# A spare fill between two gathers, no throttle in layer 1, and one activation table set, in a two-layer sparse attention kernel

## The reference

```
q = x @ Wq.T;  k = x @ Wk.T;  v = x @ Wv.T
scores = where(adj.T, q @ k.T, -1e30)
attn   = where(adj.T, softmax(scores, axis=1), 0)
x      = layernorm(x + attn @ v)          # eps 1e-5, no learned scale
```

## Time and profile before

| what | value |
|---|---|
| median of 3 runs | 311.3 us (307.36 to 314.35) |
| the profiled execution | 310.94 us, of which the span 309.1 us |
| PE busy | 186.0 us (60%) |
| ACT busy | 139.9 us (45%) |
| DVE busy | 132.5 us (43%) |
| POOL busy | 94.4 us (31%), of it 91.4 in 96 gathers |
| software DMA queue | 12.59 MB, 15.0% of 16 engines |
| mean granted PE clock | 0.797 of full |

### The profile page before, as it was taken

The page is one execution under the profiler, slowest core; times in us unless marked ns, Lnnn a source line. Parts: engine busy times, 40 slices in busy tenths (PEclk is TensorE's granted clock), DMA queues, the critical chain, the costliest instruction groups (busy, mean ns, idle before and its releaser), DMA issues.

```text
span 309.1 us, 3691 instructions
## 1 busy us (share of the span) xinstructions
PE 186.0 (60%) x1110; PEld 158.4 (51%) x1110; DVE 132.5 (43%) x671; ACT 139.9 (45%) x311; POOL 94.4 (31%) x115
## 2 busy tenths in 40 slices
PE   1739699640185879298878528650583285957640
PEld 1527587530174767197767426450473184946520
DVE  1229557010097780716874201240185063567430
ACT  1012143400124282739999772210245274688884
POOL 3457102777300036000000007776047315610000
PEclk9999685995556678879999968776599559597965
DMA  8999200433200004110011123333013204311112
GB/s 222 325 311 347 88 0 19 103 107 106 77 0 0 3 25 104 42 34 3 33 35 37 34 68 90 108 104 104 4 35 104 69 33 136 89 49 34 36 36 71
DMA packets 20982, 24.92 MB, mean 81 GB/s; under 512 B 2016, under 2 KB 17888, under 8 KB 20960
## 3 DMA queue, kind: packets, MB, share of 16 engines
q0 software_dynamic: 4608, 12.59, 15.0%
q1 hardware_dynamic: 16352, 12.06, 13.0%
HBM read 20.45 MB, written 4.19 MB: 80 GB/s over the span
## 4 chain that ended last, share of the span: by engine, by line
PE 33%; ACT 23%; issue 19%; another core or an unknown queue 16%; DVE 8%; ACTq 0%; DVEq 0%
PE PS L944 8%; PE PS L1056 7%; ACT L451 5%; PE PS L1044 3%; PE PS L1046 3%; PE PS L1009 3%; ACT first_row L424 3%; ACT exps L416 2%; PE PS L935 2%; ACT weight L435 2%; ACT L454 2%; ACT y_sb L443 2%; DVE X L775 1%; PE PS L918 1%
## 5 line engine op out<-in xcount | busy, mean ns | idle before, releaser
L1056 PE MATMUL PS<-WvT,y_sb 128*128 128x256 f32 x128 | 41.4, 456 | 33.0 <-ACT y_sb L443 32.3
L314 POOL DMA_INDIRECT xd<-x_rows,d_row x32 | 30.6, 957 | 98.6 <-DMA x_rows<-X 62.7
L1044 PE MATMUL PS<-ident,both_rows 128*128 128x128 f32 x128 | 32.6, 346 | 25.1 <-DVE both_rows L755 11.7
L944 PE MATMUL PS<-M,xt 128*128 128x256 f32 x128 | 39.5, 463 | 11.7 <-ACT xt L371 8.6
L1056 PEld LDWEIGHTS PS<-WvT,y_sb 128*128 128x128 f32 x128 | 26.0, 222 | 39.8 <-ACT y_sb L443 35.4
L775 DVE SCALAR_TENSOR_TENSOR X<-PS,inv,X 128x256 f32<-128x256 f32 x32 | 15.4, 483 | 66.9 <-PE PS L1056 62.2
L1044 PEld LDWEIGHTS PS<-ident,both_rows 128*128 128x128 f32 x128 | 26.2, 250 | 26.9 <-issue 19.5
L944 PEld LDWEIGHTS PS<-M,xt 128*128 128x128 f32 x128 | 28.4, 233 | 18.3 <-ACT xt L371 9.9
L314 POOL DMA_INDIRECT xd<-in_x,d_row x32 | 30.5, 955 | 18.5 <-DVE d_row L581 9.4
L709 DVE CUSTOM_DVE_ANT_0 prod<-Q,xd,d_none 128x256 f32<-128x256 f32 x64 | 28.4, 481 | 8.4 <-DMA xd<-x_rows,d_row 8.4
L318 POOL DMA_INDIRECT xo<-in_x,e_row x16 | 15.2, 952 | 54.5 <-DVE e_row L671 50.3
(11 more groups left out here) (125 smaller groups left out, 303.9 us busy)
## 6 DMA issues: line engine op xcount, KB each, us to landing
adj_words<-in_adj SPq DMA_DIRECT2D x4, 1024.0 KB, 7.1
X<-in_x SPq DMA_DIRECT2D x2, 1024.0 KB
x_rows<-X SPq DMA_DIRECT2D x7, 256.0 KB, 2.1
out<-X SPq DMA_DIRECT2D x7, 256.0 KB
W<-in_L_gnn_Wq SPq DMA_DIRECT2D x2, 256.0 KB
W<-in_L_gnn_Wk SPq DMA_DIRECT2D x2, 256.0 KB
xd<-in_x,d_row POOLq DMA_INDIRECT x32
W<-in_L_gnn_Wv SPq DMA_DIRECT2D x2, 256.0 KB
```

The costliest lines, as they stand in the source:

```text
L314: pool.indirect_dma_start(xd[:, t, k, :], None, rows, bass.IndirectOffsetOnAxis(ap=d_row[:, t, k:k + 1], axis=0)).then_inc(d_in[t], 16)
L944: last = nc.tensor.matmul(PS[:, 7, j * D:j * D + D], xt[:, z % 2, j, h, :], M[:, z // PAIRS, h, :], start=(h == 0), stop=(h == H - 1))
L1044: nc.tensor.matmul(PS[:, 4, at_h:at_h + P], both_rows[:, n % 2, j, h * P:h * P + P], ident[:, :], start=True, stop=False)
L1056: last = nc.tensor.matmul(projected_into(j), y_sb[:, n % 2, j, h, :], WvT[:, layer, h, :], start=(h == 0), stop=(h == H - 1))
```

## The change

Three edits. ACT loads the table set `natural_log_exp_and_others` once at the start of its program. After each gather POOL fills a spare buffer `pause`, 128x512 bf16, with zeros; each fill waits for the fill before it (`rested`). And layer 1's gathers lose the wait for products (`AHEAD` is gone).

```diff
-AHEAD = 4
...
+        pause = sb("pause", [P, BANK], BF16)
...
+            rests = {"n": 0}
+
+            def rest():
+
+                need(pool, "rested", rests["n"])
+                pool.memset(pause[:, :], 0.0).then_inc(s["rested"], 1)
+                rests["n"] += 1
+
             def direct(rows, t):
                 for k in range(S):
                     pool.indirect_dma_start(xd[:, t, k, :], None, rows,
                                             bass.IndirectOffsetOnAxis(ap=d_row[:, t, k:k + 1], axis=0)).then_inc(d_in[t], 16)
+                    rest()
 
             def overflow(rows, t):
                 pool.indirect_dma_start(xo[:, t, :], None, rows,
                                         bass.IndirectOffsetOnAxis(ap=e_row[:, t:t + 1], axis=0)).then_inc(o_in[t], 16)
+                rest()
...
             for t in range(T):
-
-                if t >= AHEAD:
-                    pool.wait_ge(s["s_done"], (S + 1) * (T + t - AHEAD + 1))
                 direct(x1_dram, t)
                 overflow(x1_dram, t)
...
+            act.preload_act_table_set("natural_log_exp_and_others")
```

More of the change, by code:

```diff
@@ L172, in edges_and_dense @@
             dist_ready own_ready own_t_ps own_t_sb l_ps listed over_ready flag m_ps m_sb xt_ps xt_sb q_ps q_sb
-            qe_ready s_done sk_in sk_ready masked topped me_ready ds_ready totalled first_in both_in p_ready a_ready
+            rested qe_ready s_done sk_in sk_ready masked topped me_ready ds_ready totalled first_in both_in p_ready a_ready
             y_ready y_sb_ready o_ready res stats spread logged rooted scaled normed normed_last x1_stored stored""".split()
```

## The result

| what | before | after |
|---|---|---|
| median, same chip (4 runs each) | 309.6 us (307.36 to 314.35) | 243.78 us (243.24 to 244.13) |
| profiled execution, its span | 310.94, 309.1 us | 243.49, 241.7 us |
| PE busy | 186.0 us (60%) | 179.0 us (74%) |
| ACT busy | 139.9 us | 97.8 us |
| DVE busy | 132.5 us | 139.5 us |

The ratio is 0.790, with a 95% interval from 0.784 to 0.795. The step that failed is the size of a term: the held signals of the start and of pair 0 stood in the sum with 20 us less 4, and 27.5 were measured. Executions of one kernel differ by a few per cent, the slower ones mostly at a lower granted clock; medians here are of all of them, ratios and intervals of the faster ones.

The account below looks back on a forecast made before the run. Bounds: partly in-line table loads and PE results reported late during unbroken gathers. Layer 1's first gather at 185.15 - 15 - 20 = 150.2, plus 85.6, 22.1, 4 and 1.8 gave 264 us; range 247 to 318.

Parts of the forecast that it names:

- the held signals of the start and of pair 0: Layer 0: PE results reported late beside gathers; freeing them gives 5 + 3 + 12, sum 20 us (bounds 12 and 23).
- The mechanism: POOL's gather sequences: a break of half a microsecond with a plain POOL instruction lets PE's late reports through; chance 0.50.
- does not free: Rival at PE's reports under gathers: fills only lengthen the sequences and signals stay held; 337 us, chance 0.17.
- half freed: Rival at PE's reports under gathers: signals pass at some fills, half the gain stays; 286 us, chance 0.21.
- 47 gathers of layer 1: POOL in layer 1: gathers set the pace at 1.76 us each, 82.7 us from first to last issue.
- landing: End of layer 1's gathers: the last gather's rows land 2.9 us after its issue.
- from the last rows to the end: Layer 1's last stretch, first product of pair 7 to end: 27.1 us less 5 of table loads, 22.1.
- The signal that waits for the gather under way: Start and pair 0: some eight signals still wait for the running gather's end, half of 0.95 on average; costs 4 us.
- The table set in layer 0: ACT in layer 0: every table load but the first goes, giving 15 us (bounds 10 and 20).
- The fourth sequence: Layer 0: a fourth sequence of 8 gathers grows by 0.5 us for each gather; no held signals counted for it.
- The fill: POOL after each gather: 512 elements take 0.51 us, partly hidden or not, so a gather every 1.76 us or so.
- the fill holds DVE: Rival in layer 0's list building: some forty short DVE operations held by fills add 10 us, 274; chance 0.03.

Follow-up runs that it names:

- the landing version: Kernel after without fills, POOL instead waiting before each tile's gathers until the rows of the tile before have landed: 256.94 us, where the kernel before took 313.1.

## Why the prediction was right in kind and 20 us off in size

**The mechanism.** On a chip with holds, the fill frees PE's signals: predicted at 0.50, and seen in both directions, since the set with a lost wait gives 305.6 and the fill added to it 243.2 on the same chip. The two kernels' 66 us are about 18 for the set (311.7, the fastest of the kernel before on chip 4, to 293.4) and 50 for the fill with the lost wait (293.4 to 243.2, over two chips). The rivals "does not free" and "half freed" fell for 512 elements. As mechanisms they exist at other lengths. With 1 element the signals are not freed, and after the last gather 64 us are left (235.17 to 299.1; the rival had 56); but the time is 304 and not 337, for a short fill doesn't lengthen the sequences, and layer 1 starts at 170.54 and not at 194. "Half freed", forecast at 286, is nearest to 256 elements, at 264.

**The terms**, in us of the profiled span:

| step of the prediction | forecast | measured | off by |
|---|---|---|---|
| start and pair 0: held signals less the 4 us of late ones | -20 + 4 = -16 | -27.5 | 11.5 |
| rest of layer 0: table loads, fourth sequence | -15 + 0 | -17.5 | 2.5 |
| 47 gathers of layer 1 | 82.7 | 79.0 | 3.7 |
| landing | 2.9 | 3.0 | -0.1 |
| from the last rows to the end | 22.1 | 19.7 | 2.4 |

Together 20 us, the difference of 264 and 243.8. The range stopped at 247 although the prediction's own bounds for its terms, added up, reach lower: 264 less 14 for a hidden fill, 5 for the table loads and 3 for the signals is 242. The marks for the first two lines are ACT's first copy of a sum, here from the kernel before:

```profile
90.00 0.60 ACT L443 ACTIVATE y_sb<-PS 128x512 f32<-128x512 f32 x1 [3.64 <-PE PS L1046]
```

and the same copy after, with two of the undisturbed stretch:

```profile
62.46 0.60 ACT L452 ACTIVATE y_sb<-PS 128x512 f32<-128x512 f32 x1 [3.64 <-PE PS L1055]
...
108.64 0.60 ACT L452 ACTIVATE y_sb<-PS 128x512 f32<-128x512 f32 x1 [1.06 <-PE PS L1055]
...
116.07 0.60 ACT L452 ACTIVATE y_sb<-PS 128x512 f32<-128x512 f32 x1 [1.07 <-PE PS L1055]
```

*The held signals* were the mis-sized term, and the step that failed. I added up three reads and stayed below their sum. Measured by the marks: POOL's overflow list is ready at 41.86 in place of 51.44, 9.6 us where I took 5 out of bounds that ended at 7; the expanded queries give another 5.4 (68.36 to 53.38 is 15.0) where I took 3; the scatter gives the 12 (83.10 to 55.91 is 27.2). So the start lost more than the one signal that I had found in the earlier trace rows. ACT's copy of the folded weight comes at 16.25 in place of 22.30; and PE's pauses, which I had not seen at all, go: the 64 matmuls of the third packing took 4.84 us before (30.36 to 35.20), with 1.2 us of "issue" twice among them, and take 1.93 after. The set alone on the two kinds of chips has its overflow list at 52.78 and at 38.26, 14.5 us apart.

*The signal that waits for the gather under way* (4 us of cost) was all but nothing. The read at 55.91 stands 0.03 us behind its matmul while a gather runs. Two reports of the packing are 2.0 and 1.6 us late, but layer 1 starts only 0.3 us later than on chip 5 (140.07, 139.75), where none is.

*The table set in layer 0* was right in size. The set alone on a chip with holds goes from its first copy at 91.44 to layer 1 in 80.8 us, before it was 95.1: 14.3 against 15. A pair takes 7.44 us (108.64 to 116.07) and not 8.61. What ends it now is PE, as the share of busy time shows (length; busy us and count of PE, PEld, DVE, ACT, POOL; granted clock; DMA share; GB/s):

```profile
100.00:135.00 35.00, 34.50 (x221) 31.24 (x220) 25.32 (x117) 23.74 (x70) 0.54 (x2) 1.00 0.13 43
```

PE works 34.5 of 35 us at the full clock (2.4 GHz), so faster ACT would give nothing more here. The Trainium skill's page "ScalarE: Activation LUTs", section "Table sets: the hidden batching unit", on which the one load rested, is confirmed: 33 loads became 1.

*The fourth sequence* of 8 gathers, which I left out, held signals too. From the first copy of a sum to layer 1 the set alone takes 80.8 us on chip 4 and 75.0 on chip 5 (62.74 to 137.75), so they were worth 5.8 there. With the fill 77.6 are left: the other 3.2 of the 17.5.

*The fill* takes 0.54 us, estimated at 0.51, and adds 0.40 to a step rather than 0.51, since 0.14 of the idle time is covered: the 3.7 us of layer 1. That the gathers would set its pace was right.

*The rival "the fill holds DVE"* had a chance of 0.03 and 10 us. It is real. Two groups of the list building, after and, in the second fence, before (count, busy us, mean ns):

```profile
L612 DVE TENSOR_SCALAR X<-top 128x128 uint32<-128x128 uint32 x2 | 1.4, 685 | 0.0
L618 DVE TENSOR_SCALAR X<-X 128x128 uint32<-128x128 uint32 x2 | 1.5, 753 | 0.0
```

```profile
L603 DVE TENSOR_SCALAR X<-top 128x128 uint32<-128x128 uint32 x2 | 0.4, 216 | 0.0
L609 DVE TENSOR_SCALAR X<-X 128x128 uint32<-128x128 uint32 x2 | 0.5, 234 | 0.0
```

With a fill of 1 element the last of them is back at 230 ns:

```profile
L618 DVE TENSOR_SCALAR X<-X 128x128 uint32<-128x128 uint32 x2 | 0.5, 230 | 0.0
```

DVE's busy time grows with the fill: 133.0 us (none, or 1 element), 134.4 (256), 137.3 (384), 138.3 (512), 148.9 (768), all on chips without holds. On the path it cost 2.7 us up to the first overflow gather (the windows above), of which 2.0 are left at layer 1's start (137.75 and 139.75). For 768 it is 9.1 and 10.3. The Trainium skill's page "SBUF — State Buffer", section "Who interferes with whom", which has VectorE and GpSimd exclude each other at a shared pair of ports, agrees with these rows. I gave its rule too little.

**What I didn't ask** is whether the held signals are this kernel's or this chip's. On chips 14, 5 and 3 the same change gives 2% (0.981, 0.970 to 0.992), of which the set gives some 11% (ratio 0.889, 0.870 to 0.908) and the fill takes most back. Neither version is best on both kinds: the set alone has 219 to 222 and 293, the kernel after 240 and 243. The lost wait is worth nothing beside the fill (241.3 kept, 240.5 dropped, over two chips), nothing clear of the spread without it on a chip without holds (219.3 to 222.3), and costs about 12 without it on one with holds (293.4 to 305.6, over two chips).

**Open:** what in a chip makes the holds, and whether a chip keeps its kind; whether PE's pauses and the late reports have one cause, and what in a stream of gathers makes either; how long a break has to be between 256 and 512 elements, and how rare it may be, since 384 wasn't run on a chip with holds and the landing version paused only after every third gather.

## What to carry to other kernels

When a reader of an engine's result starts late and the profile can't name a sender, set the end of the writer's instruction beside the read, and look for what else runs from the one to the other; here it was a stream of gathers, and a break in it, not a particular instruction, gave the time back. Look also at the writer: matmuls that wait for nothing and yet come in bits show that it is held too. Measure such a cure on more than one chip before it is kept: on top of the table set the fill was worth -50 us on one kind and +19 to +24 on the other. Where every signal of a stretch can be held, take its gain from marks at both ends of the stretch, not from the waits that you happen to have found. Before filling an engine with spare work, ask what the fill shares with its neighbours; here it held DVE's operations.

## What the runs showed of the hardware that was not expected

- Six chips fall in two groups for one kernel, 246 to 250 us and 313 to 319. In the second group PE's finished work is reported late while POOL issues gathers with 0.30 us between: by 17.9 us in the kernel before (201.01 to 218.88), by 42.9 with 48 gathers unbroken (197.06 to 239.95, chip 10). In the first group no "remote" wait stands in any of the eleven traces taken there, and in the nine of them that hold every update of PE's semaphores each stands within 0.06 us of its matmul's end.
- In the second group PE also pauses between matmuls that wait for nothing: 64 of them took 11.55 us beside gathers with fills of 256, and 1.75 on a chip of the first group. Without gathers the two groups work alike: PE 29.50 of 30 us at the full clock on both.
- The delay goes away gradually with the length of the break: 303.7, 264.1 and 243.2 us for fills of 118, 330 and 544 ns.
- A fill of 128 x N bf16 took 121, 223, 328, 437, 542 and 755 ns for N = 1, 128, 256, 384, 512 and 768, about 0.83 ns per element of a partition. The idle time ahead of a gather is 0.16 us behind a fill and 0.30 behind a gather.
- One-input DVE operations on 128x128 uint32 took up to three times as long beside fills of 512 (216 to 685 ns), and as long as ever beside fills of 1; a 128x8 conversion went from 172 to 1299 ns beside fills of 768.
